# The scale of the FFN's last layer goes into its weights, and the order of the work changes at the kernel's two ends

## The reference

```
x = x + 0.5 * ffn(layernorm(x))
x = x + attn(layernorm(x))
x = x + 0.5 * ffn(layernorm(x))

ffn(x): h = silu(x @ w1.T * s1) * (x @ w2.T * s2)      # 128 -> 512
        h = gelu(h @ h1.T * sh1)                       # 512 -> 512
        h = gelu(h @ h2.T * sh2)                       # 512 -> 512
        return h @ w3.T * s3                           # 512 -> 128, s3 one number for each output column
```

## Time and profile before

| | |
|---|---|
| median of the three runs | 1386.29 us |
| profiled execution | 1386.23 us |
| its span, first to last instruction | 1384.4 us |
| TensorE busy (matmuls) | 1351.9 us, 98% of the span |
| VectorE, ScalarE, GpSimd busy | 858.5, 663.1, 566.1 us |
| VectorE's multiplication L760 | 17 times, 691 ns for 128x512, 424 ns for 128x256 |
| TensorE's mean granted clock | 0.998 |
| HBM | 77.88 MB read, 41.94 MB written |

### The profile page before, as it was taken

How to read it: one execution, slowest core, us unless ns; L and a number is a source line. 1 busy time by engine, 2 the same in 40 slices (tenths; PEclk the granted TensorE clock), 3 DMA queues, 4 the chain that set the end, 5 groups by cost and what they waited for, 6 DMA issues and landing times.

```text
span 1384.4 us, 25270 instructions
## 1 busy us (share of the span) xinstructions
PE 1351.9 (98%) x9792; PEld 929.6 (67%) x9792; DVE 858.5 (62%) x2503; ACT 663.1 (48%) x1130; POOL 566.1 (41%) x644
## 2 busy tenths in 40 slices
PE   8999999999999999999999999999999999999998
PEld 4456676658856587566875568655786658855887
DVE  4477976466774577744766558656586446775542
ACT  2476646236642456425662356622666236642233
POOL 0038343822447144560437515283144823466000
PEclk9999999999999999999999999999999999999999
DMA  6030255432564144630447315463254432640000
GB/s 187 27 97 1 82 132 115 89 81 70 130 130 94 41 100 125 133 90 30 122 99 141 89 30 125 113 108 89 61 134 101 88 74 83 141 106 31 9 1 8
DMA packets 346471, 121.47 MB, mean 88 GB/s; under 512 B 312624, under 2 KB 327728, under 8 KB 346352
## 3 DMA queue, kind: packets, MB, share of 16 engines
q1 hardware_dynamic: 346352, 119.86, 37.1%
HBM read 77.88 MB, written 41.94 MB: 87 GB/s over the span
## 4 chain that ended last, share of the span: by engine, by line
PE 71%; issue 9%; DVE 7%; POOL 7%; DMA 2%; ACT 2%; SPq 1%; POOLq 0%; DVEq 0%; ACTq 0%
PE bank L1466 23%; PE bank L1582 9%; PE bank L1495 4%; PE bank L1677 4%; PE bank L1668 4%; PE bank L1641 3%; PE bank L1607 3%; PE bank L1474 3%; PE bank L1658 3%; POOL blkT L613 2%; PE bank L1632 2%; POOL blkP L610 2%; PE bank L1649 2%; PE bank L1624 2%; PE bank L1890 1%
## 5 line engine op out<-in xcount | busy, mean ns | idle before, releaser
L1466 PE MATMUL bank<-big,h 128*128 128x512 f32 (+1 forms) x1056 | 444.2, 569 | 0.0
L1466 PEld LDWEIGHTS bank<-big,h 128*128 128x128 f32 x1056 | 194.8, 190 | 191.8 <-issue 185.8
L567 POOL TENSOR_TENSOR rnorm<-ssq,mhalf 128x16 f32<-128x16 f32 (+1 forms) x35 | 84.1, 2404 | 426.4 <-DVE ssq L877 426.4
L1582 PE MATMUL bank<-wqkv,nT 128*128 128x512 f32 x336 | 160.0, 597 | 1.1 <-ACT V L1285 1.1
L613 POOL TENSOR_TENSOR blkT<-blkT,blkP 128x31 f32<-128x31 f32 (+15 forms) x248 | 135.3, 545 | 19.4
L610 POOL TENSOR_TENSOR blkP<-blkA,blkT 128x31 f32<-128x31 f32 (+15 forms) x248 | 129.3, 522 | 29.5 <-DMA blkA<-blocks_out 10.7
L1495 PE MATMUL bank<-xT,w 128*128 128x512 f32 (+1 forms) x272 | 118.6, 579 | 8.7 <-DVE big L753 5.9
L1195 ACT ACTIVATE big<-bank,cols 128x512 f32<-128x512 f32 (+1 forms) x68 | 43.9, 662 | 133.9 <-PE bank L1466 95.8
L1203 ACT ACTIVATE big<-bank,cols 128x512 f32<-128x512 f32 (+1 forms) x68 | 44.1, 662 | 126.1 <-PE bank L1466 126.1
L1002 DVE TENSOR_TENSOR MT<-bank,MT 128x512 f32<-128x512 f32 x56 | 38.5, 691 | 100.4 <-PE bank L1624 100.4
L594 POOL TENSOR_TENSOR QET<-QET,sgf 128x1024 f32<-128x1024 f32 x24 | 56.5, 2354 | 98.3 <-DMA sgf<-e_rows 91.1
(11 more groups left out here) (239 smaller groups left out, 2433.4 us busy)
## 6 DMA issues: line engine op xcount, KB each, us to landing
rows_or_g<-g_rows SPq DMA_DIRECT2D x28, 512.0 KB, 5.0
q_rows<-mid SPq DMA_DIRECT2D x28, 512.0 KB, 4.7
QET<-q_rows SPq DMA_DIRECT2D x112, 128.0 KB, 4.2
k_rows<-R SPq DMA_DIRECT2D x27, 512.0 KB, 2.7
KT<-k_rows SPq DMA_DIRECT2D x108, 128.0 KB, 3.8
sgf<-e_rows SPq DMA_DIRECT2D x24, 512.0 KB, 4.5
blocks_out<-R SPq DMA_DIRECT2D x128, 32.0 KB, 1.7
blkA<-blocks_out SPq DMA_DIRECT2D x8, 512.0 KB, 3.8
```

The source lines that it names most:

```text
L567: pool.tensor_tensor(rnorm[:, heads_of], ssq[:, heads_of], mhalf[:, :].to_broadcast([128, heads_of.stop - heads_of.start]), ALU.pow).then_ ...
L1466: last = pe.matmul(bank[bk + i][:, t], w[:, k, 128 * o:128 * o + 128], src[:, k, t], start=(k == 0), stop=(k == KB - 1))
L1582: pe.matmul(bank[proj_bank(b, n)][:, :], nT[:, 128 * c:128 * c + 128], wqkv[:, i // 2, 512 * (i % 2):512 * (i % 2) + 512], start=True, sto ...
```

## The change

1. VectorE multiplies `w3` by the halved `s3row` once, after the weights have landed (semaphore `c_w3`, for which TensorE waits once, before the first last-layer product). `result` is one addition from PSUM, which signals `sc`; the semaphore `res` goes.
2. The second and third DMA of the first batch row are issued by ScalarE, after its wait for GpSimd's constants; idle products 16 become 20.
3. First row's joins: VectorE does the statistics of the keys' squares before it copies join 3's output and the rest of the sums after it; the rows `n0` move behind the new state, `unit_k(1, 0)` moves ahead of the clearing of the blocks and the new state. The last of the projections done ahead comes behind join 3 on TensorE and ScalarE.
4. Last row's joins: VectorE does both `turn_T1` before join 0's output, and both late `turn_R` before join 1's output. Idle products 20 become 27.

```diff
-            load_xin(0)
+            sp.dma_start(xin[:, FIRST, :], rows_of(d["x"], 0)[:, FIRST, :]).then_inc(ld_x, 16)
...
             def store(b, chunks=WHOLE, n=None):
-                sp.wait_ge(F["f2"]["res"], (b if n is None else n) + 1)
+                sp.wait_ge(F["f2"]["sc"], (b if n is None else n) + 2)
...
                 dve.wait_ge(f["l4"], b + 1)
-                dve.tensor_tensor(xn[:, k, :], heads(bank[4])[:, k, :], s3row[:, :].unsqueeze(1).to_broadcast([128, len(chunks), D]),
-                                  ALU.mult).then_inc(f["sc"], 1)
-                dve.wait_ge(f["sc"], b + (2 if n == "f2" else 1))
-                dve.tensor_tensor(x[:, k, :], xn[:, k, :], x[:, k, :], ALU.add).then_inc(f["res"], 1)
+                dve.tensor_tensor(x[:, k, :], heads(bank[4])[:, k, :], x[:, k, :], ALU.add).then_inc(f["sc"], 1)
...
             def joins_alone():
                 turn_T(0), turn_R(0, 1), gates_abs(1), turn_R(0, 3), joined(0, 0)
                 turn_R(0, 0), joined(0, 1), gates_log(1)
-                turn_R(0, 2), joined(0, 2), cumulated(1), joined(0, 3)
-                squares(1, 0), N_rows(1, n0, 0, n_n0)
+                turn_R(0, 2), joined(0, 2), cumulated(1), squares_stats(1, 0), joined(0, 3), squares_sums(1, 0)
...
             def SP_first(s, p):
+                if p == 1:
+                    unit_k(p, 0)
                 if p is not None:
                     unit_blocks(p)
                 new_state(s, 0, 0)
                 if p is not None and p > 1:
                     squares(p, 0)
                 new_state(s, 0, 1)
-                if p is not None:
+                if p == 1:
+                    N_rows(1, n0, 0, n_n0)
+                elif p is not None:
                     unit_k(p, 0)
                 attended(s, 0)
...
             dve.wait_ge(F["f2"]["sc"], 1)
+            dve.tensor_tensor(w3[:, :, :], w3[:, :, :], s3row[:, :].unsqueeze(1).to_broadcast([128, KB, D]), ALU.mult).then_inc(c_w3, 1)
...
-            turn_T(B - 1), turn_R(B - 1, 1), turn_R(B - 1, 3), joined(B - 1, 0), turn_T1(1), turn_T1(3)
-            joined(B - 1, 1), turn_R(B - 1, 2), turn_R(B - 1, 0), joined(B - 1, 2), joined(B - 1, 3)
+            turn_T(B - 1), turn_R(B - 1, 1), turn_R(B - 1, 3), turn_T1(1), turn_T1(3), joined(B - 1, 0)
+            turn_R(B - 1, 2), turn_R(B - 1, 0)
+            for k in range(1, JOINS):
+                joined(B - 1, k)
...
                 joined(0, 2)
-                for c, i in AHEAD[8:]:
-                    silu(1, c, i)
-                joined(0, 3)
+                silu(1, *AHEAD[8]), joined(0, 3), silu(1, *AHEAD[9])
...
             act.wait_ge(c_pool, 1)
+            first_rows = d["x"][0:1, :, :].rearrange("o (c p) n -> p (o c) n", p=128)
+            for p, r, k in ORDER[1:]:
+                act.dma_start(xin[p, k, :], first_rows[r, k, :]).then_inc(ld_x, 16)
...
                 else:
+                    if (n, b, k) == ("f1", 0, 0):
+                        pe.wait_ge(c_w3, 1)
                     pe.wait_ge(f["g3"], b * KB + k + 1)
...
-                    idle_products(bank[3], 20)
+                    idle_products(bank[3], 27)
...
                 lone_join(2), N_sums(1)
-                for c, i in AHEAD[8:]:
-                    proj(1, c, i)
-                lone_join(3)
+                proj(1, *AHEAD[8]), lone_join(3), proj(1, *AHEAD[9])
...
-            idle_products(bank[7], 16)
+            idle_products(bank[7], 20)
```

More of the change, by code:

```diff
@@ L277, in ffn_sems @@
         def ffn_sems(n):
-            names = ("tr", "xT", "gate", "silu", "hid", "l2", "g2", "l3", "g3", "l4", "sc", "res")
+            names = ("tr", "xT", "gate", "silu", "hid", "l2", "g2", "l3", "g3", "l4", "sc")
             return {k: sem(f"{n}_{k}") for k in names}
@@ L298, in build_program @@
         warm, act_warm = ez[:, 0:1], sem("act_warm")
-        c_swap = sem("c_swap")
+        c_swap, c_w3 = sem("c_swap"), sem("c_w3")
         a_TB, a_unit_v = sem("a_TB"), sem("a_unit_v")
@@ L787, in N_moments @@
                 s = ln_n
-                dve.wait_ge(F["f1"]["res"], b + 1)
+                dve.wait_ge(F["f1"]["sc"], b + 1)
                 moments(s, b, x1, 0.0)
@@ L863, in squares, with squares_stats @@
             def squares(b, g):
+                squares_stats(b, g), squares_sums(b, g)
+            def squares_stats(b, g):
                 lo, hi = H if g == NC else 0, H if g == 0 else 2 * H
@@ L869, in squares, with squares_sums @@
                 last.then_inc(p_bst, 1)
+            def squares_sums(b, g):
+                lo, hi = H if g == NC else 0, H if g == 0 else 2 * H
                 k = (b - 1) * NG + g
```

## The result

| | before | after |
|---|---|---|
| median (lowest to highest), 8 runs each | 1386.81 (1383.34 to 1390.1) us | 1391.44 (1389.45 to 1392.42) us |
| ratio, 95% interval | | 1.0032 (1.0024 to 1.0041) |
| profiled execution, its span | 1386.23, 1384.4 us | 1390.62, 1388.9 us |
| TensorE's mean granted clock | 0.998 | 0.996 |

The changed kernel is slower by 4.6 us. The forecast was 1382.7 us with a range to 1386.4: wrong. The page after first: TensorE and VectorE, and the two kinds of queue that moved data by the issuing engines. q10 is new; it carries the 0.13 MB of the two half loads that ScalarE now issues.

A forecast was written before the change was run, and what follows sets the result against it. TensorE bounds the kernel (busy 1351.9 of 1384.4 us); VectorE's work counts only at the ends. -0.6 - 0.45 + 1.2 - 2.3 - 2.8 = -5.0 us, 1381.3; 1382.7 with one likely clock fall; range 1380.0 to 1386.4.

The forecast's parts named there:

- Part 2, the first load: At the beginning: the last half load lands at 5.2 to 5.85, costing +0.9 to +1.5 us, taken as +1.2.
- far bound: At the beginning: the last half load lands behind h1T, at 10.0, +5.7 us; dropped because of the separate rings.
- The second rival: At the beginning: the first row's second half queues behind h1T, delay 5.7 instead of 1.2, 1387.2 us; chance 0.08.
- one of two places where a fall could come: Idle stretches at the beginning and before slot 13: one clock fall there, +1.2 to +1.7 us, likelier than none.
- They end at 8.9: At the beginning: the 4 more idle products take 0.9 us, end at 8.9 before the transposes and cost nothing.
- only two pieces of work that ran at 1.2 GHz: Between 1236 and 1291 us: the only half-clock work, both falls just after TensorE stood without products for about 2 us.
- Part 1: Scale in the weights: -0.6 us after the first FFN and -0.45 us at the end, nothing in the loop.
- Part 3: First row's joins: keys stored 3.2 us earlier, wait before L1607 gone (2.6 us), solve 0.3 us later; together -2.3 us.
- Part 4: Last row's joins: VectorE's chain without a hole brings L1641 at 1288.0 instead of 1290.81, gain 2.8 us.
- The third rival: First row's joins: the wait for the keys stays because store, load or GpSimd don't come earlier, 1385.3 us; chance 0.08.
- The first: Last joins: the gain is the clock's and falls in both new idle stretches give it back, 1384.2 us; chance 0.2.
- I am wrong if the loop changes: Middle loop: turns were to stay at 165.8 to 166.2 us; any change there was a sign against the forecast.

The follow-up runs named there:

- held kernel: The changed kernel, but SyncE issues h1T and the loads behind it only when all of the first x has landed: 1384.75 us, ratio 0.9991.
- ScalarE's early issues: The changed kernel with ScalarE's two issues put ahead of its wait for GpSimd's constants: 1382.67 us, ratio 0.9971.
- x on SyncE: The changed kernel with all three loads of the first batch row issued by SyncE again, 20 idle products kept: 1382.37 us, ratio 0.9971.
- 44 idle products: The changed kernel with 44 instead of 20 idle products at the beginning: 1390.39 us, ratio 1.0030 against the kernel before.
- the old order's join: The changed kernel with all first-row loads on SyncE and the last row's turns in the old order: 1386.60 us, ratio 0.9988.

## Why the prediction was wrong

- **Part 2, the first load: the step that failed.** "so the last half goes out at 2.95 and lands at 2.95 + 2.24 = 5.2 at the least; with the latency of w1T and w2T, its new neighbours, 2.9, at 5.85." It went out at 3.13 and landed at 10.18. The latency was taken from neighbours that are issued ahead of `h1T` with nothing large under way; this half is issued 0.39 us behind `h1T`, and the load that resembles it in that is `h1T` itself. That was my far bound (lands at 10.0, +5.7), and it was right to 0.2 us. "Against it: w1T and w2T, sent behind x, needed only 2.9" was no evidence, since neither was sent behind anything big. The held kernel comes near what I had forecast: 3.1 us, and a landing at 6.23, still 0.4 past my upper figure.
- The Trainium skill (DMA: Bandwidth & Descriptors, Queues, rings and completion order) says that ScalarE and SyncE own a ring each and that an engine alternates between rings; from it I concluded that a small load in a second ring isn't held up by a large one in the first. The runs contradict the conclusion: 7.1 us from issue to landing behind `h1T` in the other ring, 3.1 without it. The page's other sentence (section Issuing engines are not separate DMA queues), that issuing from a second engine saves only issue time, agrees: ScalarE's early issues were worth 0.05 us.
- **The second rival** is what happened, at a chance of 0.08. Its time, 1387.2, was still 4.2 us short. It had the landing and left out what that does to TensorE: the pause of 5.38 us and the half clock behind it, 2.96 us in the profile. My own sum named the beginning as one of two places where a fall could come and priced it for 16 products that begin 1.2 us later; a wait that becomes longer has to be priced with the clock that it brings. Beside it stand the loop's +1.34 and the fall at 155.2 (the stretch with it took 21.05 us, 0.76 longer than with x on SyncE), and against them the 1.4 us that 1382.7 holds for one fall.
- **Idle products.** "They end at 8.9": they ended at 9.97 (7.61 us for 40, where the same 40 took 6.58 with x on SyncE). The first products of every kernel are 0.21 us apart and the later ones 0.11, as the transposes of half and of full clock are, so my "only two pieces of work that ran at 1.2 GHz" left these out. The pace changed at 8.4 us in the changed kernel, at 6.3 with x on SyncE, and anywhere from 5.8 to 8.4 in the 14 profiled executions, in kernels that begin alike too. In the same window TensorE did 19 products with x on SyncE and 11 in the changed kernel:

```profile
6.40:8.30 1.90, 1.90 (x19) 1.00 0.79 191
```

```profile
6.40:8.30 1.90, 1.90 (x11) 1.00 1.02 383
```

  It cost nothing, as TensorE then stood for 5.38 us.
- **Part 1** was right in place and size where I looked for it (-0.68 and -0.48 against -0.6 and -0.45). The new product took 0.69 us at 27.73 us, hidden as forecast.
- **Part 3** was right in mechanism: statistics in VectorE's hole, store of the keys 2.9 us nearer to the solve (6.29 us behind it with x on SyncE, 9.19 before; forecast 3.2, and 2.4 if measured from turn_T), no wait before the keys' products. The size was off by a factor near two (-1.25 against -2.3), because the wait of 2.42 us was the longest of six executions of the same order (0.62 to 2.42).
- **Part 4** was right in mechanism; forecast from turn_T to the solve 26.1 us, measured 25.8 to 26.8. The -2.8 counted in full a fall of the clock that two of six executions of the old order have in that place; the part measured -1.35 by the medians, -2.1 by the ratio.
- **The third rival** (the keys' wait stays) fell for the keys that it meant: no wait before them in any of the kernels with the new order. But six of these eight, the changed kernel among them, wait 0.76 to 1.54 us for the next row's keys instead, which neither the sum nor a rival had. **The first** (the clock gives it back) fell too, as above.
- **The loop.** I took its length of before as given. In the 13 other profiled executions the five turns took 830.4 to 832.6 us whatever the edit, and the 829.84 of before was the shortest of all. The +1.34 and +1.84 of the table are not all luck of that one execution, though: the first turn is longer wherever the new wait stands. "I am wrong if the loop changes" was the right sign to watch.

**What is best.** The change with x on SyncE, or with ScalarE's two issues moved ahead of its wait: 1382.37 and 1382.67 us, both 0.9971 of before, and some 8.5 us below the change as it stood (1.0032).

## What to carry to other kernels

Price a moved load by what has been issued ahead of it and just behind it, in any queue, and not by the latency of small loads that happen to be near it. Here a second queue didn't shield it, and an issue that waits for something unrelated (here ScalarE's for the constants) can slip behind the first big one. If a load on the critical path comes late, add what TensorE's clock takes for the pause: half of the busy time in the stretch at 1.2 GHz. Measure the parts together as well as alone: two of them had a wait between them that neither has by itself. And where a forecast hangs on one wait of one execution, look whether the same wait recurs with the same length elsewhere; a single profile of this kernel carried about 2 us of luck.

## What the runs showed of the hardware that I had not expected

- A half of 64 KB on a second queue took 7.1 us from issue to landing behind a 1 MB load on the first, and 3.1 with that load and those after it held back.
- Behind pauses of 5.38, 7.10 and 8.27 us at the start TensorE was at half clock for 6.8, 10.2 and 10.2 us; behind one of 2.00 us (held), with the transposes after it, it was not. Other falls of 3.4 us came in some executions at 59.1, 67.6, 147.6, 154.5 or 155.2 us and in others of nearly the same instructions not at all. I found no row of before that would have told which.
- An addition of 128x512 with both inputs in SBUF took 1.91 to 1.99 us while GpSimd was at work, and 0.68 at the same place with one input in PSUM.
- A store of 512 KB took 4.4 to 5.0 us to land where a load of instructions fell into it, and 2.7 to 2.9 at the same place where none did.
- TensorE can stop for about 2 us between two equal small products without a releaser in the trace: 2.16 us at 154.84 (44 idle products) and 1.78 us in the old order's join, in each case in one execution. A load of instructions (q8) had begun 0.5 and 0.7 us ahead of the pause, at 152.21 and 1276.04; whether it is the cause was not tested, and other such loads had no pause behind them.

```profile
1278.49 0.21 PE L2000 MATMUL bank<-R,TB 32*32 32x32 f32 x1 [1.78 <-issue]
```
